# Last attention: row maxima from one product of the scores, turned scores from three

## The reference, cut to what matters

```python
q = q.reshape(b, t, h, dh).transpose(0, 2, 1, 3)
k = k.reshape(b, t, h, dh).transpose(0, 2, 1, 3)
v = v.reshape(b, t, h, dh).transpose(0, 2, 1, 3)
attn = jnp.einsum('bhqd,bhkd->bhqk', q, k) * scale
attn = jax.nn.softmax(attn, axis=-1)
attn_out = jnp.einsum('bhqk,bhkd->bhqd', attn, v)
```

## Time and profile before

| what | us |
|---|---|
| median of 3 runs (lowest, highest) | 2036.42 (2035.14, 2037.17) |
| the profiled execution | 2036.34 |
| its span, from the first to the last instruction | 2034.6 |
| TensorE busy in the span | 1728.0 |
| VectorE busy | 1585.6 |
| ScalarE busy | 1251.1 |
| GpSimd busy | 348.9 |

### The profile page before, as it was taken

The page is one execution under the profiler, slowest core; times in us unless marked ns, Lnnn a source line. Parts: engine busy times, 40 slices in busy tenths (PEclk is TensorE's granted clock), DMA queues, the critical chain, the costliest instruction groups (busy, mean ns, idle before and its releaser), DMA issues. The chain is left out here.

```text
span 2034.6 us, 46173 instructions
## 1 busy us (share of the span) xinstructions
PE 1728.0 (85%) x16491; PEld 1083.0 (53%) x16498; DVE 1585.6 (78%) x3793; ACT 1251.1 (61%) x3209; POOL 348.9 (17%) x464
## 2 busy tenths in 40 slices
PE   5999969846859999947759999999968999999585
PEld 5999944435633444425544444444436666665453
DVE  4444459878878999967878999999967787777774
ACT  5666637723526655555438888888856666665465
POOL 1000001000011111110001212222113443443211
PEclk7555569978968999978989999999979999999798
DMA  3000007210004443300006666666620000000100
GB/s 79 10 4 4 4 15 271 88 43 1 0 14 171 154 171 149 141 17 1 0 12 232 232 232 225 224 226 229 232 87 22 22 1 22 21 1 1 36 2 22
DMA packets 51670, 174.06 MB, mean 86 GB/s; under 512 B 7104, under 2 KB 32448, under 8 KB 34112
## 3 DMA queue, kind: packets, MB, share of 16 engines
q1 hardware_dynamic: 50368, 170.09, 23.3%
q10 hardware_dynamic: 1152, 1.90, 0.3%
HBM read 167.45 MB, written 2.95 MB: 84 GB/s over the span
## 5 line engine op out<-in xcount | busy, mean ns | idle before, releaser
L861 DVE TENSOR_TENSOR ps<-ps,m_comb 128x512 f32<-128x512 f32 x520 | 363.1, 699 | 23.9 <-DMA m_comb<-m_shares 7.2
L846 DVE TENSOR_TENSOR m_hwlo<-ps,m_hwhi 128x512 f16<-128x512 f32 x520 | 353.5, 680 | 0.3
L822 ACT ACTIVATE m_hwhi<-ps 128x512 f16<-128x512 f32 x520 | 308.3, 593 | 20.8 <-DVE ps L861 19.4
L828 ACT ACTIVATE ps<-ps 128x512 f32<-128x512 f32 x388 | 225.9, 582 | 80.7 <-PE ps L778 80.5
L778 PE MATMUL ps<-x_hi,m_whi 128*128 128x512 f16 x652 | 250.3, 384 | 8.2 <-DVE m_hwlo L846 4.2
L778 PE MATMUL ps<-x_lo,m_whi 128*128 128x512 f16 x652 | 250.0, 383 | 0.0
L778 PE MATMUL ps<-x_hi,m_wlo 128*128 128x512 f16 x652 | 249.7, 383 | 0.0
L759 POOL CAST m_whi<-m_stage 128x256 f16<-128x256 f32 (+1 forms) x130 | 55.2, 424 | 907.2 <-PE ps L784 637.6
L461 DVE TENSOR_TENSOR rn_s_lo<-rn_s_full,rn_s_hi 128x32 f16<-128x32 f32 x512 | 98.4, 192 | 131.5 <-ACT rn_s_full L418 131.5
L784 PE MATMUL ps<-m_hwhi,m_whi 128*128 128x512 f16 x520 | 197.4, 380 | 0.3 <-DVE m_hwlo L846 0.2
L784 PE MATMUL ps<-m_hwlo,m_whi 128*128 128x512 f16 x520 | 197.3, 379 | 0.0
(11 more groups left out here) (451 smaller groups left out, 3983.8 us busy)
## 6 DMA issues: line engine op xcount, KB each, us to landing
m_comb<-m_shares SPq DMA_DIRECT2D x128, 1024.0 KB, 5.1
m_stage<-in_m_w SPq DMA_DIRECT2D x97, 128.0 KB, 4.6
m_stage<-in_m_w SPq DMA_DIRECT2D x33, 192.0 KB, 4.7
lj_w<-in_lj_w SPq DMA_DIRECT2D x6, 1024.0 KB, 5.1
lq_w<-in_lq_w SPq DMA_DIRECT2D x1, 1600.0 KB, 6.9
la_w<-in_la_w SPq DMA_DIRECT2D x1, 1280.0 KB, 5.3
rn_rows<-in_L_attn_rows SPq DMA_DIRECT2D x4, 256.0 KB, 4.5
rn_xs<-rn_xn_hi SPq DMA_DIRECT2D x32, 32.0 KB, 1.9
```

The source lines that it names most:

```text
L822: nc.scalar.activation(hw_hi[:, k % HB, :], weighted(k), ACT.Copy).then_inc(hi_done, 1)
L828: nc.scalar.activation(acted(k), ps[:, 4, :] if gated else bank(k), func).then_inc(act_done, 1)
L846: nc.vector.tensor_tensor(hw_lo[:, k % HB, :], weighted(k), hw_hi[:, k % HB, :], ALU.subtract)\
L861: nc.vector.tensor_tensor(weighted(k), bank(k), comb[:, s, n * QW:(n + 1) * QW], ALU.mult)\
```

## The change

The scores have one product in place of three, high by high, so that a step has two rounds of scores. The row maxima are taken from that. The turned scores keep their three products and the negated maximum. The scores now wait for the high parts of q and k, and the turned scores get the waits for the low parts.

```diff
                 for i in range(TB):
-                    for left, right in ((q_hi, k_hi), (q_hi, k_lo), (q_lo, k_hi)):
-                        out.append([(ps[:, bank + j, i * T:(i + 1) * T], left[r, m, a, t0 + i * P:t0 + (i + 1) * P],
-                                     right[r, m, a, t0:t0 + T], left is q_hi and right is k_hi, left is q_lo)
-                                    for j, r in enumerate(rows)])
+                    out.append([(ps[:, bank + j, i * T:(i + 1) * T], q_hi[r, m, a, t0 + i * P:t0 + (i + 1) * P],
+                                 k_hi[r, m, a, t0:t0 + T], True, True) for j, r in enumerate(rows)])
                 return out
...
                     if score % 2 == 0 and b % 2 == 0:
-                        pe.wait_ge(q_lo_s, 2 * (b // 2) + a + 1)
-                        pe.wait_ge(k_lo_s, 2 * (b // 2) + a + 1)
+                        pe.wait_ge(q_hi_s, 2 * (b // 2) + a + 1)
+                        pe.wait_ge(k_hi_s, 2 * (b // 2) + a + 1)
...
                 if turn is not None:
+                    b, a, _ = heads(turn)
+                    if turn % 2 == 0 and b % 2 == 0:
+                        pe.wait_ge(q_lo_s, 2 * (b // 2) + a + 1)
+                        pe.wait_ge(k_lo_s, 2 * (b // 2) + a + 1)
                     pe.wait_ge(neg_on, turn // 2 + 1)
                     wait(pe, exp_s, turn)
                     turneds = turned_rounds(turn)
```

## The result

| | before | after |
|---|---|---|
| median (lowest, highest), 7 runs each | 2036.42 (2033.97, 2037.62) | 2043.42 (2042.37, 2046.22) |
| ratio | | 1.0032, 95% interval 1.0022 to 1.0041 |
| profiled execution | 2036.34 | 2046.22 |
| span | 2034.6 | 2044.4 |
| first score of the last attention starts | 1917.12 | 1920.11 |

I had forecast no change, 2036.3 us. The change made the kernel slower. In the profiled executions the stage itself is 6.88 us longer, about the 7.0 us of the medians. The profiled execution happens to be the slowest of its seven: another 3.0 us lie ahead of the first score, where the two kernels have the same instructions. In the 14 traces of this study the first score begins anywhere between 1915.4 and 1920.2.

The account below looks back on a forecast made before the run. TensorE's order of work and its waits were taken to set the pace. Rounds, steps 0 to 2, maxima, waits and GpSimd each counted 0, so 2036.34 gave 2036.3 us; likeliest case 2033.0 to 2039.8.

Parts of the forecast that it names:

- Rounds beside turned rounds cost no time: Steps 3 to 31: removing four of six score rounds changes TensorE by 0 us, since eight turned rounds remain.
- points 1 and 2: Score matmuls removed in steps 3 to 31, then in steps 0 to 2: 0 us each, the latter bounded by -1.3.
- Steps 0 to 2: No turned scores there: TensorE done 1.3 us earlier together, none passed on because VectorE is late; 0, bounds 0 and -1.3.
- Maxima: Row maximum on VectorE can start 0.44 us earlier in 12 steps; slack absorbs it: 0, bounds 0 and -5.3 us.
- The pauses that remain: TensorE's pauses for VectorE's output addition (2.1 us in 5 places) and low parts of q and k: nothing moves them.
- The waits: Turned scores gain two waits at 8 places, values long there: 0 us, other bound 1.2 us.
- GpSimd: Earlier small conversion on VectorE falls within GpSimd's multiplication; VectorE waits, so 0 us, bounds 0 and +0.8.
- Rival C: Stage start: TensorE's clock falls to its lower level from step 2 to step 6; +5.8 us, 2042.1 us; 4 in 100.

Follow-up runs that it names:

- pairs 3 to 7: The kernel before with one product of the scores in pairs 3 to 7 alone, waits as before: 2040.5 us, ratio 1.0017.
- The kernel with the layer norm alone filled: The kernel before plus 85 small TensorE matmuls, results unread, in the layer norm that opens the stage: 2038.0 us, ratio 1.0006.

## Why the prediction was wrong, step by step

1. **Rounds beside turned rounds cost no time: right as to time, wrong as to what they do.** A step from 7 to 12 is the same to 0.01 us with two rounds as with six. But this was put as "0 us on TensorE", and the sum counted only a step's length. This is the step that failed: points 1 and 2 priced the missing matmuls by their time at a clock of 1.00, and what they do for the clock stood in none of the terms, only in a rival. The runs showed 4.5 us in its place from step 2 to step 5, and up to 1.8 more at the end.
2. **Steps 0 to 2: the direct effect right.** VectorE works its list from the same start, and the pause ahead of the transposes is 1.10 us (0.9 forecast).
3. **Maxima: right.** The places where the maximum waits for the scores fell from 12 with 12.1 us to 9 with 10.0, and each of the waits in steps 9, 17 and 25 from 1.49 to 1.05 us, the 0.44 forecast; the line of who waited, for the earlier trace rows:

```profile
  DVE lq_neg L2221: 10.0, 9
```

   No step from 7 on came sooner by it. Steps 15, 23 and 31 win back 0.03 or 0.04 us each, but so they do in the kernel that only adds the waits, and not with the waits put back.
4. **The pauses that remain: right**, step by step, from step 7 on, but for what the waits add.
5. **The waits: taken at 0, measured at 0.15 to 0.32 us** at steps 5, 13, 21 and 29, about 0.6 in all, inside the bound of 1.2 us. At steps 3, 11 and 19 they cost nothing, at 27 0.03. I had compared the passed waits of step 10, where TensorE comes straight from matmuls; at the four costly places it stands idle until `neg_on` (0.67 us ahead of step 13, 0.85 ahead of step 29), and there the further waits show. Rows of the wrong kind of place.
6. **GpSimd: right.** The conversion takes up to 758 ns, the multiplication 1262 to 1281 as before, for the earlier trace rows:

```profile
L2229 DVE CAST lq_negparts<-lq_neg x16: 185/186/758, 1924.5 to 2011.9; 128x8 bf16<-128x8 f32 x16
...
L2210 POOL TENSOR_TENSOR lq_o<-lq_u,lq_rec x8: 1262/1278/1281, 1947.8 to 2026.6; 128x512 f32<-128x512 f32 x8
```

   It is VectorE that waits: in step 13 the conversion ends at 1961.63, the multiplication, which began before it, at 1961.59. The Trainium skill, GPSIMD Engine Reference, property table ahead of section 1.1, says that the two share their interfaces to SBUF. The trace agrees, with 0.61 us for a conversion of 0.19 and an unchanged 1.28 for the multiplication.

**Rival C happened**, at the place that I gave and at a price not far off: 4.5 us up to step 6 against 5.8. That the whole came as near as 2043.4 against 2042.1 is in part luck, since C left out the waits and the end. It also blamed the 1.3 us missing from steps 0 to 2 alone; by the trace with those steps changed and no others, that is 2.0 of the 4.5 us, and the rounds missing beside turned ones make the rest. I gave C 4 in 100 for two reasons, and both were bad. The stretch from 2010.00 to 2013.00 with TensorE busy 44% at full clock was one stretch of one execution; at the end of the stage the clock fell 3 us sooner (96.6 to 96.8 us from the first score) in three other kernels with six rounds there. And "the time in which TensorE is busy at all doesn't shrink" measured the wrong thing: 8 of the 28 small matmuls of a steady step were gone at no loss of busy time, and that by itself loses the clock (pairs 3 to 7, 5.38 us busy against 5.39).

The Trainium skill, TensorE: Matmul & The Clock Gate, Part 1 (The HAM clock gate), says that the lower clock is the default and that activity lifts it. The trace of the kernel before agrees: 0.50 from 1904.00 to 1911.50, with TensorE busy 0.31 of 7.50 us, then 3.18 us of work from 1911.50 to 1914.70, then 1.00. The last part of the same page of the Trainium skill (Why this matters for your kernels) has it as a rule to leave no long pauses between matmuls. That wasn't enough here: the clock was lost with no pause of TensorE over 1.6 us in steps 0 to 2.

Of the 6.9 us of the stage, then: 4.5 are the clock in steps 2 to 5, 0.6 the waits, 1.8 the end. Some of the last may be chance: the two kernels with six rounds and added waits lost 1.2 there against the one profile of before, with a clock that fell 3.3 us sooner, so that I can only say that between 0.6 and 1.8 belongs to the change. That isn't settled, nor is what makes each of the late falls happen in one execution and not in another.

## What to carry to other kernels

Matmuls that run beside others in other rows of the array were free by the timeline here, and without them the clock fell. Before taking such work out, look at the pauses in that stretch, and price a fall of the clock as a term of its own: it can be several times the time that was "saved" (1.3 us of work taken from steps 0 to 2 cost 4.5 us by the medians). The cheapest test is to issue the remaining matmul again in place of the removed ones. Two more waits that were already met cost nothing where TensorE came straight from other matmuls, and 0.15 us or more where it stood idle at a wait.

## What I had not expected of the hardware

- Falls of the clock lie at a few instants from the first score that several kernels share (4.4 to 4.5, 7.8 to 7.9, 76.3, 96.6 to 96.8, 100.0 to 100.1 us), though the stage's start varies by 4.7 us against the span's. The kernel with the layer norm alone filled has others, and the fall at 89.9 us stands alone. The first rise is at 18.1 or 18.2 us whether the clock fell at 4.5 or at 7.8, in all five kernels with fewer rounds in steps 3 to 5 and no filling. So delayed work can cross a fall that stays where it is, as at the end of the changed kernel.
- Two rounds less of six did as much harm as four, 2044.6 against 2043.4 us.
- Medians can hide it: with one product in pairs 8 to 31 the median is 2.2 us up, and the slowest run is 15 us up. A profile of one execution can mislead the other way.
